# Local layers: where the second phase of the values product stands in the order of TensorE

## The reference

```
qkv = shift_tokens(x) @ Wqkv            # 16 heads of 64
q, k = l2norm(q)*qs, l2norm(k)*ks, then rotated by position
sim  = q @ k^T * 8 over windows of 32 queries and 64 keys, masked
attn = softmax(sim)
out  = attn @ v                          # the values product
x    = out @ Wo + x
x    = (a * gelu(gate)) @ W2 + b2 + x    # from layernorm(shift_tokens(x)) @ W1 + b1
```

## Time and profile before

| | us |
|---|---|
| median of 3 runs | 2784.53 |
| lowest and highest | 2778.47 and 2786.81 |
| the profiled execution | 2770.18 |
| its span, first to last instruction | 2768.3 |
| TensorE matmul busy | 2393.4 |
| VectorE busy | 1983.0 |
| ScalarE busy | 1761.3 |
| GpSimd busy | 1476.9 |

### The profile page before, as it was taken

The page is one execution under the profiler, slowest core; times in us unless marked ns, Lnnn a source line. Parts: engine busy times, 40 slices in busy tenths (PEclk is TensorE's granted clock), DMA queues, the critical chain, the costliest instruction groups (busy, mean ns, idle before and its releaser), DMA issues. The chain is left out here.

```text
span 2768.3 us, 94039 instructions
## 1 busy us (share of the span) xinstructions
PE 2393.4 (86%) x35312; PEld 1682.9 (61%) x35340; DVE 1983.0 (72%) x3067; ACT 1761.3 (64%) x3659; POOL 1476.9 (53%) x1060
## 2 busy tenths in 40 slices
PE   7999867896456787758999999999999999999994
PEld 4777545665343444336777677777777677777773
DVE  5888653222226888767888888888888888888872
ACT  4666532333126766546777887788777887788772
POOL 2444324222222445456767777777767777777760
PEclk9999978988777999889999999999999999999996
DMA  9100005871320000101122112211121211121120
GB/s 333 42 0 0 13 23 163 233 216 33 94 81 1 0 0 0 47 24 32 31 64 50 30 30 53 61 30 45 46 50 33 53 46 32 44 61 38 30 46 16
DMA packets 143198, 153.92 MB, mean 56 GB/s; under 512 B 12240, under 2 KB 111632, under 8 KB 141840
## 3 DMA queue, kind: packets, MB, share of 16 engines
q1 hardware_dynamic: 139024, 144.53, 19.3%
q0 software_dynamic: 4096, 8.40, 1.0%
HBM read 75.29 MB, written 27.26 MB: 37 GB/s over the span
## 5 line engine op out<-in xcount | busy, mean ns | idle before, releaser
L2382 POOL TENSOR_TENSOR c<-a,bq 128x1024 f32<-128x1024 f32 x192 | 453.9, 2364 | 235.9 <-DVE bq L2447 235.4
L2392 POOL TENSOR_TENSOR qn<-c,ss 128x1024 f32<-128x1024 f32 x192 | 378.1, 1969 | 28.7 <-issue 3.7
L2031 PE MATMUL ps<-wqk,xs 128*128 128x512 f32 x768 | 370.7, 606 | 18.9 <-POOL xs L2375 18.1
L2446 DVE TENSOR_TENSOR a<-ps,tab 128x512 f32<-128x512 f32 x384 | 262.9, 685 | 13.1 <-ACT sq L2221 7.9
L2400 POOL TENSOR_TENSOR z<-z,sm 128x1024 f32<-128x1024 f32 x96 | 182.8, 1904 | 148.5 <-DVE sm L2475 148.5
L2447 DVE TENSOR_TENSOR bq<-ps,tab 128x512 f32<-128x512 f32 x384 | 261.3, 680 | 0.0
L2221 ACT ACTIVATE sq<-ps 128x512 f32<-128x512 f32 x384 | 215.5, 597 | 61.8 <-PE ps L2031 61.7
L2454 DVE TENSOR_REDUCE ss<-sq 128x16 f32<-128x1024 f32 x192 | 230.5, 1217 | 31.3 <-issue 16.6
L1426 POOL TENSOR_TENSOR hC<-hs,Cs 128x1024 f32<-128x1024 f32 x64 | 150.4, 2355 | 177.3 <-ACT Cs L1571 90.7
L2031 PEld LDWEIGHTS ps<-wqk,xs 128*128 128x128 f32 x768 | 139.8, 192 | 143.6 <-issue 138.8
L2042 PEld LDWEIGHTS ps<-ident,qn 128*128 128x128 f32 x1536 | 177.5, 142 | 71.4 <-issue 42.9
(11 more groups left out here) (307 smaller groups left out, 5374.7 us busy)
## 6 DMA issues: line engine op xcount, KB each, us to landing
Vw<-Vs SPq DMA_DIRECT2D x192, 256.0 KB, 4.0
win_rows<-rows_q SPq DMA_DIRECT2D x24, 256.0 KB, 3.3
outs_q<-win_out SPq DMA_DIRECT2D x24, 256.0 KB, 2.8
wqk<-in_wqkv SPq DMA_DIRECT2D x6, 1024.0 KB, 5.0
leaves<-in_f_w SPq DMA_DIRECT2D x9, 576.0 KB, 4.4
leaves<-in_q_w SPq DMA_DIRECT2D x1, 4608.0 KB, 18.8
leaves<-in_k_w SPq DMA_DIRECT2D x1, 4608.0 KB, 22.6
leaves<-in_v_w SPq DMA_DIRECT2D x8, 576.0 KB, 4.4
```

The costliest lines, as they stand in the source:

```text
L2031: nc.tensor.matmul(jobs.out(n), xs[:, t * 128:(t + 1) * 128], wqk[:, (2 * y + s) * 512:(2 * y + s + 1) * 512], start=True, stop=True).then ...
L2382: nc.gpsimd.tensor_tensor(f(c), f(a), f(bq), ALU.add).then_inc(c_ready.sem, 1)
L2392: nc.gpsimd.tensor_tensor(qn[:, t, y, :, :, :].rearrange("p h s e -> p h (s e)"), c[:, y, :, :, :].rearrange("p h s e -> p h (s e)"), spre ...
L2446: nc.vector.tensor_tensor(a[:, y, :, s, :], Zs, spread(table(0, s), H1), ALU.mult)
```

## The change

The second phase of step m is issued in body it directly behind the first phase, ahead of OUT2. It is taken out of the next body, where it stood between Z00 and Z01. All other orders stay as they are: ScalarE, VectorE, GpSimd and SyncE wait for the same semaphores at the same places.

```diff
                     do(front, pair("Z00"), project, 0, 0)
-                    if late:
-                        end_values(n)
                     do(front, pair("Z01"), project, 0, 1)
                     do(mid, pair("T11"), turn, m, 1, 1)
                     do(late, ("WO",), outputs, n)
...
                     do(front, pair("S0"), scores, 0)
                     do(mid, VALUES, begin_values, m)
+                    if mid:
+                        end_values(m)
                     do(late, ("OUT2",), hidden_out)
```

## The result

| | before | after |
|---|---|---|
| median of the timed runs, us | 2782.46 (6 runs, 2774.05 to 2787.43) | 2806.59 (6 runs, 2802.05 to 2811.80) |
| ratio to before, 95% interval | | 1.0091 (1.0076 to 1.0107) |
| the profiled execution, us | 2770.18 | 2802.09 |
| its span, us | 2768.3 | 2800.3 |
| period of the loop, us | 31.10 | 31.54 |

The forecast was 2804.7, with the body longer by 0.44 us; the body grew by 0.43. The page's busy times and then the table by stretches answer to the earlier trace rows; TensorE still runs at the full granted clock (2.4 GHz) there.

The account below looks back on a forecast made before the run. TensorE's own order was taken to set the period in the local layers. 46 x 0.44 = 20.2 us, with edges summing to 0, carried to the timed median of 2784.53 gave 2804.7 us (+0.7%), range 2788 to 2822.

Parts of the forecast that it names:

- (d): ScalarE's squares of Z00 stand ahead of its four copies, so WO starts 0.24 + g later, 0.44 us a body.
- (f): Code outside the loop: +3.7 us in the body ahead, -4 in the body behind, sum 0 with 4 either way.
- (a): Phase 2 waits exposed for the end of phase 1, beginning at phase 1 + 1.57 + g.
- g: Time from the modelled end of phase 1's last matmul to phase 2's first, taken as 0.20 us.
- The rival with 0.81: Long wait before phase 2, g like 0.81: 1.05 us a body, +48, 2833 us; chance 0.06.
- (b): Z00 and Z01: two fewer changes of tiling mode a body, both groups become 1.72 us, 0.19 back.
- (c): TensorE alone, phase 1 to T11: 8.03 us becomes 7.90 + g, +0.07 a body.
- One sign: Idle time of about 0.2 us before T11 or WO, put down to ScalarE's oT.
- (e): Other engines' chains still fit: Z01's bank by 0.21 us, VectorE before WO by 0.17, qn for T00 by 0.18.
- the rival of code supply: Scores and both phases, some 800 instructions, stop 1.26 us in every pass: +58, 2842 us; chance 0.04.
- the forecast of 20.2: Loss over the loop in us: 46 bodies at 0.44 each, with the edges at 0; chance 0.70.

Follow-up runs that it names:

- both orders altered: Changed kernel with ScalarE's copies ahead of the squares of Z00 and VectorE's sums ahead of adding OUT2; ratio 1.0037 to the kernel before, period 31.13 us.
- the first experiment: Changed kernel with ScalarE's four copies of the values ahead of the two squares of Z00; ratio 1.0082 to the kernel before, period 31.46 us.

## Why the prediction was right

The mechanism was the one forecast: ScalarE, with its squares ahead of the copies, holds WO. The body's 0.44 was met by 0.43, but two errors inside it cancel (d), and the total came near with the help of terms that were not in the sum (f). Point by point, in one body; all of after is read from the rows above.

(a) The exposed wait. g = 0.20 was taken; it is 0.16 to 0.17. The rival with 0.81 was far off, as the drain and six instructions in it suggested.

(b) Changes between small tiles and whole-array matmuls. Right: from Z00 to T11, with nothing late, it is 3.43 (both orders altered), twice 1.72, where Z00 and Z01 took 1.81 and 1.82. The 0.19 is real.

(c) TensorE alone: 8.90 + 0.07 was forecast with g = 0.20; the kernel with both orders altered has 8.94, a period of 31.13.

(d) ScalarE. The four copies were to end at phase 1 + 8.91 + g = 9.08 with the measured g; they end at 1939.84, which is 9.10. The size of the travel time was off: WO starts 0.13 after the last copy, not 0.23, so at 9.23 where 9.31 would have been (T11 starts only 0.05 after the second copy, whose bank it needs). What was not in the sum made up for it: WO takes 3.55 to the next group, not 3.46, as its first weight load, held by the wait, starts with its first matmul (1939.96 and 1939.97) and no longer 0.10 ahead of it (1948.80 and 1948.90 before). 0.33 and 0.09 give 0.42, and 0.01 more stands ahead of phase 1. That 0.44 was met so closely is luck; the sizes in it were right to 0.1 only. One sign was not seen in the form named: TensorE's matmuls show no idle time before T11 or WO, because modelled ends overlap it. The hold is in the distances (T11 to WO 1.06, where it was 0.87) and in the weight load's line. That ScalarE holds WO is shown by the extra square, which costs its full 0.48 here and nothing before.

(e) The covers held, two of them more narrowly than computed. qn was to come 1.77 later in the body and came 1.76 later; T00 was to have 0.18 to spare, but no travel time was counted there, and with 0.13 of it 0.04 is left. Z01's bank is freed at 1936.55, and its first weight load, which runs a matmul ahead, starts at 1936.66 in its usual spacing. That is 0.11 behind, where 0.53 was counted (0.32 of travel and 0.21 left). The step says that any of these chains pays an excess; it does not say what the first experiment showed, that they also take over when ScalarE's goes.

(f) The edges were mis-sized. They were put at 0 with 4 either way. In the two profiled executions, from phase 1 of body 1 to WO of the first pass it is 12.90 before and 16.66 after (+3.8, where +3.7 was forecast, though from other parts); the first pass, WO to WO, is 32.54 and 37.29, +4.8 of which the steady period explains 0.4; from the last pass's phase 1 to the end it is 81.8 and 81.1, -0.7 where -4 was forecast. Five groups of TensorE after: in body 1, in the first pass (two), and twice in body 49.

```profile
1263.34 0.48 PE L2099 MATMUL ps<-pT,Vw 32*64 32x32 f32 x5 [1.82 <-issue]
...
1301.26 0.72 PE L2099 MATMUL ps<-pT,Vw 32*64 32x64 f32 x31 [1.92 <-issue]
1301.91 2.86 PE L2164 MATMUL ps<-hid,w 128*128 128x256 f32 x6
...
2755.45 0.52 PE L2099 MATMUL ps<-pT,Vw 32*64 32x64 f32 x16 [1.71 <-issue]
...
2761.64 5.58 PE L2129 MATMUL ps<-oT,wo 128*128 128x256 f32 x16 [2.82 <-PEq L2024]
```

The first pass of the loop stops in mid-phase too, and the second phase in it stops like the first does; this was left out. By the rows, stops in body 1 come 128 weight loads and 128 matmuls apart. That agrees with the blocks of 256 instructions of "Runtime: NRT & Kernel Launch", section Instruction fetch mechanics, in the Trainium skill. From the second pass on there is no such stop, so the rival of code supply was right for one pass of 46 and wrong for the others. (The view of the earlier trace rows has a second instruction queue besides the one shown, with 2 packets before and 1 after; and the rival's 2842 is the 58 us alone, without the half of (d) that it names.)

The stops are not all of it: the granted clock of TensorE falls behind them. Two stretches of the kernel before, the first pass with its stop and what follows it, and then the first pass of after with its stops (from:to, length, busy times of the engines, then PEclk, DMA share, GB/s):

```profile
1258.90:1290.00 31.10, 29.33 (x636) 21.92 (x636) 23.96 (x38) 24.02 (x50) 20.47 (x14) 1.00 0.16 36
1291.00:1312.00 21.00, 21.00 (x346) 14.69 (x345) 17.75 (x27) 16.61 (x38) 13.88 (x9) 1.00 0.22 50
```

```profile
1291.00:1312.00 21.00, 16.81 (x432) 12.36 (x431) 11.16 (x19) 10.97 (x23) 7.89 (x7) 0.84 0.23 52
```

Before, the one stop of 1.26 in that pass left the clock at its full level of 2.4 GHz. After, behind a stop of 1.51 and around one of 1.92, it is at the lower level of 1.2 GHz for some 7 of these 21 us. There OUT2 takes 2.86, where it takes 1.56 in other passes, and the 97 matmuls ahead of the second stop take 1.70, where 97 took 1.24 before. That is some 2 of the +4.8 us. All seven profiled kernels with the phases directly behind each other show this fall in the first pass. Of the five others, one does, for half as long. Behind body 1 it is the same: the eight projection matmuls of Z00 and Z01 take 6.55 after, in place of 3.60, while before only Z00's four were at the lower level (3.77). So a part of what a stop costs is the slower clock behind it, and no term of the sum had that. At the end, WO does not wait for the copies any more but for TensorE's own skipped steps, 2.82, so the gain expected there is not had.

The sum: 45 x 0.434 = 19.5 for the windows inside the loop, and edges of 3.8 + 4.3 - 0.7 = 7.4, give 27. The spans differ by 32.0; the other 5.0 lie ahead of phase 1 of body 1 (1250.27 and 1255.26), mostly in layers that the change does not touch, and the medians differ by 24.1. So the forecast of 20.2 had its main term right, came near the 24.1 of the medians, and would have missed the profiled execution by 12 us (2790.4 against 2802.09). How much of the edges is in the medians is not settled, since single executions of one kernel vary by 10 us. That variation goes with the mean granted clock (after, 2802.05 us at 0.938 and 2811.8 at 0.935), and the loop has no part in it: from 1300 to 2690 us the clock is 1.00 in both traces.

## What to carry to other kernels

When one engine sets the period and its order is changed, add up the way through the changed window for that engine, and then for every chain that starts in it and comes back to it, with the order of the other engines: work made ready earlier gains nothing if its consumer has something else to do first. Chains within a few tenths of each other must be shortened together before most of it is seen. Code that runs for the first time, at a loop's edges and in its first pass, needs a sum of its own; here the edges were about a quarter of the local layers' loss, stops and the clock behind them. Look also at the idle time that no engine releases: where small instructions leave no lead, each wait ahead of them costs its issue time, and it can be moved behind a long matmul, though never ahead of the event that it waits for.

## What the runs showed of the hardware

A semaphore wait that is long satisfied costs TensorE about 0.06 us when it stands between groups of small matmuls (six waits gone, 0.38 less; seven gone, 0.51 less), and nothing that shows behind the 12 matmuls of F (two waits moved there, no idle time ahead of S0). A wait of TensorE for its own last matmul, with one increment, costs 0.17 beyond the modelled end. The end of the loop and the waits ahead of Z00 cost 0.34 of idle time when 128 small matmuls stand last in the body, and nothing that shows behind six of 128x256. TensorE started 0.05 (T11) and 0.13 (WO) after the profiled end of the ScalarE copy that it waited for, and 0.13 after GpSimd's qn. With two stops of 1.51 and 1.92 us among small matmuls the granted clock was at its lower level for some 7 us, where with one stop of 1.26 it stayed at the full level.
